# Two families of 128x128 transposes moved from the tensor engine to transposing DMAs, in a one-core layer with sorted expert rows

## What is computed

```python
xn = layernorm(x)                                   # over the 128 channels
# attention part: every token picks 8 heads x 4 points of channel indices
off = xn @ W_off + b_off                            # only off[..., 0] is used
w = softmax(xn @ W_attn + b_attn)                   # over the 4 points
idx = clip(wrap_negative(int(off[..., 0])), 0, 127)
g = take_along_axis(xn[:, 0, :], idx)               # values of token 0 of each sequence
s = sum(g * w over 32 picks)                        # one number per token
attn = broadcast(s, 128) @ W_out + b_out
# feed-forward part: 2 shared experts on all tokens, 8 routed experts, 2 per token
ffn(v, w1, w2, w3) = (silu(v @ w1.T) * (v @ w3.T)) @ w2.T      # hidden size 256
out = x + attn + sum of both shared experts + weighted sum of the 2 chosen experts
```

## Time and profile before

| | us |
|---|---|
| median of 3 runs | 472.09 |
| lowest and highest | 469.29, 472.75 |
| profiled execution, device time | 468.98 |
| its span in the profile | 467.2 |

### The profile page before, as it was taken

How to read it: one execution, slowest core, us unless ns; L and a number is a source line. 1 busy time by engine, 2 the same in 40 slices (tenths; PEclk the granted TensorE clock), 3 DMA queues, 4 the chain that set the end, 5 groups by cost and what they waited for, 6 DMA issues and landing times.

```text
span 467.2 us, 13518 instructions
## 1 busy us (share of the span) xinstructions
PE 402.0 (86%) x4741; PEld 344.9 (74%) x4741; DVE 344.9 (74%) x1093; ACT 202.7 (43%) x353; POOL 198.4 (42%) x169
## 2 busy tenths in 40 slices
PE   0554776797899999999969899999999999999990
PEld 0543634464567777777847799999999999999990
DVE  5976899979848689999998778886555555555551
ACT  3797753147222554554524334543333433333330
POOL 0432404144865434333360000001888876666664
PEclk9976898799999999999979999999999999999996
DMA  8600000010241111111120144542455554432332
GB/s 301 179 2 1 1 1 1 0 36 20 81 138 44 53 32 49 54 53 46 53 54 0 34 134 133 154 130 84 61 73 65 61 72 55 67 29 27 31 29 22
DMA packets 34998, 28.75 MB, mean 62 GB/s; under 512 B 5632, under 2 KB 28544, under 8 KB 34944
## 3 DMA queue, kind: packets, MB, share of 16 engines
q1 hardware_dynamic: 23248, 19.23, 14.3%
q0 software_dynamic: 11264, 8.69, 13.1%
q10 hardware_dynamic: 432, 0.11, 0.1%
HBM read 15.13 MB, written 12.88 MB: 60 GB/s over the span
## 4 chain that ended last, share of the span: by engine, by line
PE 72%; DVE 16%; ACT 6%; issue 3%; POOL 1%; DMA 1%; POOLq 0%; ACTq 0%; DVEq 0%
PE pY L750 16%; PE pY L576 10%; PE pAB L723 8%; PE pAB L725 7%; PE pAB L724 7%; PE pAB L561 5%; PE pAB L562 5%; PE pAB L563 5%; ACT units L788 4%; PE pV L601 3%; PE pV L588 3%; PE pV L699 2%; DVE hbuf L1079 2%; DVE hot L1233 1%; ACT xT L796 1%
## 5 line engine op out<-in xcount | busy, mean ns | idle before, releaser
L957 POOL DMA_INDIRECT out_dram<-xT,rows x64 | 99.0, 1547 | 104.5 <-DVE xT L1395 67.4
L723 PE MATMUL pAB<-hotT,wsp 128*128 128x128 f16 x620 | 108.5, 219 | 0.5
L725 PE MATMUL pAB<-hotT,wsp 128*128 128x128 f16 x620 | 108.5, 219 | 0.0
L724 PE MATMUL pAB<-hotT,wsp 128*128 128x128 f16 x620 | 108.4, 219 | 0.0
L942 POOL DMA_INDIRECT sorted_rows<-rows,slot x64 | 68.2, 1066 | 84.5 <-DVE hbuf L1079 65.9
L1344 DVE SCALAR_TENSOR_TENSOR hbuf<-pAB,units 128x512 f32<-128x512 f32 x78 | 53.7, 688 | 67.4 <-PE pAB L725 65.9
L906 ACT ACTIVATE units<-pAB 128x512 f32<-128x512 f32 x78 | 46.4, 595 | 102.9 <-PE pAB L725 102.7
L750 PE MATMUL pY<-wsp,hbuf 128*128 (+1 forms) x620 | 87.0, 282 | 1.0 <-DVE xT L1406 0.7
L852 ACT ACTIVATE units<-pAB 128x512 f32<-128x512 f32 x64 | 38.1, 597 | 114.2 <-PE pAB L563 114.2
L750 PEld LDWEIGHTS pY<-wsp,hbuf 128*128 128x128 f32 x620 | 75.6, 192 | 1.9 <-DVE hbuf L1344 0.8
L576 PE MATMUL pY<-wsp,hbuf 128*128 128x128 f32 x512 | 72.0, 286 | 0.0
(11 more groups left out here) (153 smaller groups left out, 596.4 us busy)
## 6 DMA issues: line engine op xcount, KB each, us to landing
rows<-sorted_rows SPq DMA_DIRECT2D x32, 137.0 KB, 2.4
base<-in_x SPq DMA_DIRECT2D x8, 512.0 KB, 7.4
out_dram<-base SPq DMA_DIRECT2D x16, 256.0 KB, 2.6
wraw<-in_wall SPq DMA_DIRECT2D x10, 256.0 KB, 2.8
proj<-sorted_rows SPq DMA_DIRECT2D x27, 68.5 KB, 1.9
wsp<-in_wall SPq DMA_DIRECT2D x10, 128.0 KB, 3.3
sorted_rows<-rows,slot POOLq DMA_INDIRECT x64
out_dram<-xT,rows POOLq DMA_INDIRECT x64, 3.3
```

The source lines that it names most:

```text
L723: pe.matmul(o, hi, x(0), start=True, stop=False)
L724: pe.matmul(o, hi, x(1), start=False, stop=False)
L725: mm = pe.matmul(o, lo, x(0), start=False, stop=True)
L957: pool.indirect_dma_start(out_rows, bass.IndirectOffsetOnAxis(ap=xr[:, job.step, t % 2, DEST:DEST + 1].bitcast(U32), axis=0), yt[:, t], No ...
```

## The change

All transposes after stage 1 go to DMAs with a transpose, all of them issued by SyncE.

- Stage 3: `turn_hot` and `hot_copy` are gone. For each pair SyncE issues one DMA that reads 128x1024 float16 of `hot` in SBUF and writes 8 transposed blocks to `hotT`, now 4 buffers deep (`TURNS`) and laid in `units`. Number m waits for its batch of `hot` and until picks 0 to m-4 are done. `pick` lags two units and alternates between two banks of pV; `weigh` lags two units, and `weighted_high` one. The loads of expert weights stand between these DMAs in SyncE's program.
- Stage 4: a step's load is two DMAs: the 9 words of weights and destination, and a transposing DMA of 256x256 float16 from HBM straight to `xrT`. An extra load is likewise a small one and a transposing one of 128x256. Both pairs count on the same semaphore. `r_turn` and `r_xt` are gone, the lags are 0 and 2, and the transposed rows stay for good: there is no ring. SyncE's 8-ahead rule now waits for the first products of the last job of the turn 8 back (`d_l1`), not for its transposing.

The diff, cut to what is spoken of:

```diff
         share = sb("share", [P, P], F16)
-        units = sb("units", [P, 4, 512], F32)
+        units = sb("units", [P, 6, 512], F32)
         silu = units[:, 0:2, :]
-        xs = units[:].rearrange("p r (j c) -> p r j c", j=TPB)
+        xs = units[:, 0:4, :].rearrange("p r (j c) -> p r j c", j=TPB)
+        hotT = units[:, 2:6, :].bitcast(F16)
         hbuf = sb("hbuf", [P, 4, 512], F32)
...
-        hotT = sb("hotT", [P, 2, 8 * P], F16)
         for name, a in const.items():
...
-        xr = rows[:].rearrange("p (r k) w -> p r k w", k=2)
-        xrT = hotT[:].rearrange("p i c -> p (i c)").rearrange("p (r k s c) -> p r k s c", r=RING, k=2, s=2)
-        xe = proj[:].bitcast(I32).rearrange("p t c -> p (t c)")[:, 0:EXTRAS * ROWW].rearrange("p (a w) -> p a w", w=ROWW)
+        row_words = rows[:].rearrange("p t w -> p (t w)")
+        proj_words = proj[:].bitcast(I32).rearrange("p t c -> p (t c)")
+        xr_flat = row_words[:, 0:TILES * CW].bitcast(F16)
+        xrT = xr_flat.rearrange("p (r s k c) -> p r s k c", r=MAIN_STEPS, s=2, k=2)
+        meta = row_words[:, TILES * CW:TILES * ROWW].rearrange("p (t m) -> p t m", m=META)
+        xe_flat = proj_words[:, 0:EXTRAS * CW].bitcast(F16)
+        xeT = xe_flat.rearrange("p (a s c) -> p a s c", a=EXTRAS, s=2)
+        extra_meta = proj_words[:, EXTRAS * CW:EXTRAS * ROWW].rearrange("p (a m) -> p a m", m=META)
         yt = xT[:].bitcast(F32).rearrange("p i s (t c) -> p (i s t) c", c=P)
...
-        small = sb("small", [P, RING, P], F32)
+        small = sb("small", [P, 4, P], F32)
         vscr = small[:].rearrange("p (t r) c -> p t (r c)", t=2)
...
-        xr16 = xr.bitcast(F16)
-        xr32 = xr.bitcast(F32)
-        xe16 = xe.bitcast(F16)
-        xe32 = xe.bitcast(F32)
+        meta32 = meta.bitcast(F32)
+        extra_meta32 = extra_meta.bitcast(F32)
         pV16 = pV[:].bitcast(F16)
-        pT16 = pV16[:, :, 0:4 * P].rearrange("p b (k s c) -> p b k s c", k=2, s=2)
...
             before = sum(1 if s < MAIN_STEPS else min(2, EXTRAS - 2 * (s - MAIN_STEPS)) for s in TURN_ORDER[n % AHEAD:n + 1:AHEAD])
-            eng.wait_ge(d_in[n % AHEAD], 16 * before)
-
-        def rows16_of(job, k):
-
-            return xr16[:, job.step, k] if job.main else xe16[:, 2 * job.i + k]
+            eng.wait_ge(d_in[n % AHEAD], 16 * 2 * before)
...
                 sp.dma_start(second[:, :, e, :], wall[e, :, W2:WCOL].rearrange("p (h c) -> p h c", h=2)).then_inc(w2_ready, 16)
-            with sp.Fori(1, NE // 2) as g:
-                for r in range(2):
-                    sp.wait_ge(w_split, 2 * g + r - 1)
-                    sp.dma_start(wraw[:, r, 0:W2], wall[bass.ds(2 * g + r, 1), :, 0:W2].rearrange("o p w -> p (o w)")
-                                 ).then_inc(w_in[r], 16)
+
+            def load_first(e):
+
+                sp.dma_start(wraw[:, e % 2, 0:W2], wall[e, :, 0:W2]).then_inc(w_in[e % 2], 16)
+
+            for e in range(NSH, 2 * NSH):
+                sp.wait_ge(w_split, e - 1)
+                load_first(e)
+            for m in range(APAIRS):
+                if m % 4 == 0:
+                    sp.wait_ge(hot_ready, m // 4 + 1)
+                if m >= TURNS:
+                    sp.wait_ge(v_done, m + 1 - TURNS)
+                sp.dma_start(hotT[:, m % TURNS].rearrange("p (k c) -> p k c", c=P),
+                             hot[:, m // 4 % 2, 2 * (m % 4):2 * (m % 4) + 2].rearrange("p s g b h -> p (s g b h)"),
+                             transpose=True).then_inc(hot_turned[m % TURNS], 16)
+                if m % 4 == 3 and 2 * NSH + m // 4 < NE:
+                    e = 2 * NSH + m // 4
+                    sp.wait_ge(w_split, e - 1)
+                    load_first(e)
...
                     at = nc.s_assert_within(sp.snap(tile), 0, TILES - 1, skip_runtime_bounds_check_because="clamped")
-                    sp.dma_start(xe[:, a - 1], sorted_tiles[bass.ds(at, 1)].rearrange("o p w -> p (o w)")).then_inc(landed, 16)
+                    sp.dma_start(extra_meta[:, a - 1], sorted_tiles[bass.ds(at, 1), :, CW:ROWW].rearrange("o p m -> p (o m)")).then_inc(landed, 16)
+                    sp.dma_start(xeT[:, a - 1], sorted_tiles16[bass.ds(at, 1), :, 0:2 * P].rearrange("o p c -> p (o c)"),
+                                 transpose=True).then_inc(landed, 16)
...
-                    sp.wait_ge(d_turn, n + 1 - AHEAD)
+                    sp.wait_ge(d_l1, LAST_OF_TURN[n - AHEAD] + 1)
                 if step < MAIN_STEPS:
-                    sp.dma_start(xr[:, step], sorted_steps[step]).then_inc(d_in[n % AHEAD], 16)
+                    sp.dma_start(meta[:, 2 * step:2 * step + 2], sorted_steps[step][:, :, CW:ROWW]).then_inc(d_in[n % AHEAD], 16)
+                    sp.dma_start(xrT[:, step].rearrange("p s k c -> p s (k c)"), sorted_halves[step][:, 0:2 * P],
+                                 transpose=True).then_inc(d_in[n % AHEAD], 16)
                 else:
...
-            def turn_hot(g, u):
+            def pick(g, u):
                 m = ROUND * (g - ATT) + u
-                if u % 4 == 0:
-                    pe.wait_ge(hot_ready, 2 * (g - ATT) + (u // 4 + 1))
-                if past(m, 1):
-                    pe.wait_ge(hotT_ready, m)
-                for k in range(2 * NG):
-                    mm = pe.transpose(pV16[:, 0, k * P:(k + 1) * P],
-                                      hot[:, u // 4, 2 * (u % 4) + k // NG, k % NG].rearrange("p b h -> p (b h)"),
-                                      c["ident"][:])
-                mm.then_inc(hot_turned, 1)
-
-            def pick(g, u):
-
-                m = ROUND * (g - ATT) + u
-                pe.wait_ge(hotT_ready, m + 1)
-                if past(m, 1):
-                    pe.wait_ge(v_read, m)
+                pe.wait_ge(hot_turned[u % TURNS], 16 * (2 * (g - ATT) + u // TURNS + 1))
+                if past(m, 2):
+                    pe.wait_ge(v_read, m - 1)
                 for k in range(2 * NG):
                     for s in range(2):
-                        mm = pe.matmul(pV[:, 1, k * 64:(k + 1) * 64], hotT[:, u % 2, k * P:(k + 1) * P],
+                        mm = pe.matmul(pV[:, u % 2, k * 64:(k + 1) * 64], hotT[:, u % TURNS, k * P:(k + 1) * P],
                                        table[:, bass.ds(2 * (g - ATT) + u // 4, 1), s, :].rearrange("p o c -> p (o c)"),
...
             routing = shared[:1] + [(0, routing_products, 0, UNITS)] + shared[1:]
-            both = shared[:1] + [(0, turn_hot, ROUND * ATT, UNITS), (1, pick, ROUND * ATT, UNITS)] + shared[1:]
+            both = shared[:1] + [(2, pick, ROUND * ATT, UNITS)] + shared[1:]
             straight(0, 2 * ROUND, routing)
...
-            def r_turn(g, r):
-
-                job = JOBS[UNROLL * g + r]
-                if not job.turns:
-                    return
-                rows_landed(pe, job.step)
-                if job.turn == 0:
-                    pe.wait_ge(w_split, NE)
-                if job.turn >= 2:
-                    pe.wait_ge(d_xt, job.turn - 1)
-                for k in range(2 if job.main else job.experts):
-                    for s in range(2):
-                        mm = pe.transpose(pT16[:, job.turn % 2, k, s, :], rows16_of(job, k)[:, s * P:(s + 1) * P], c["ident"][:])
-                mm.then_inc(d_turn, 1)
-                if job.turn == 0:
-                    spread_sides()
-
             def r_first(g, r):
...
-                pe.wait_ge(d_xt, job.turn + 1)
+                if q == 0:
+                    pe.wait_ge(w_split, NE)
+                    spread_sides()
+                if job.turns:
+                    rows_landed(pe, job.step)
                 if q >= 2:
...
-                        x = lambda s: xrT[:, job.turn % RING, job.t % 2 if job.main else k, s, :]
+                        x = lambda s: xrT[:, job.step, s, job.t % 2, :] if job.main else xeT[:, 2 * job.i + k, s, :]
                         for h in range(2):
...
-            def hot_copy(g, u):
-                m = ROUND * (g - ATT) + u
-                act.wait_ge(hot_turned, m + 1)
-                if past(m, 2):
-                    act.wait_ge(v_done, m - 1)
-                nc.scalar.copy(hotT[:, u % 2, :], pV16[:, 0, :]).then_inc(hotT_ready, 1)
-
             def routed_high(g, u):
...
-            def r_xt(g, r):
-
-                job = JOBS[UNROLL * g + r]
-                if not job.turns:
-                    return
-                act.wait_ge(d_turn, job.turn + 1)
-                if job.turn == 0:
-                    act.wait_ge(v_done, APAIRS)
-                if job.turn >= RING:
-                    act.wait_ge(d_l1, LAST_OF_TURN[job.turn - RING] + 1)
-                n = 2 if job.main else job.experts
-                nc.scalar.copy(xrT[:, job.turn % RING, 0:n], pT16[:, job.turn % 2, 0:n]).then_inc(d_xt, 1)
-                if job.turn == 0:
-                    act.wait_ge(sides_done, 1)
```

(36 more changed lines are left out.)

6 lines of the change are left out of this document (1 added, 5 removed).

## The result

| | before | after |
|---|---|---|
| median, us | 470.92 (469.29 to 472.75, 4 runs) | 479.24 (478.48 to 479.59, 4 runs) |
| profiled execution, its span | 468.98, 467.2 | 479.59, 477.5 |
| ratio after to before | | 1.0173, 95% interval 1.0126 to 1.0221 |

The account below looks back on a forecast made before the run. TensorE was taken to set the pace in stages 3 and 4; gains of 8.0 us (stage 3) and 10.1 us (stage 4), 18.1 in all, off 470.8 gave 452.7, stated as 452.5 us. Range 444 to 550, the likeliest case's own 444 to 461.

Parts of the forecast that it names:

- the DMA part: Bounds on the added transposing DMAs in stages 3 and 4: 1.9 to 2.9 us a pair, hidden, costing nothing.
- the turning point: Stage 4's extra turns: SyncE's issue time per transposing DMA above which it would turn bad, 0.95 us.
- the extra turns: Stage 4, 14 turns of extra tiles: 0.22 us saved each; SyncE 2.2 us behind, covered by 18 us head start.
- Stage 3: One-hot transposes leave TensorE and VectorE sets the pace at 3.0 us in units 36 to 59: 8.0 us gained.
- the seam: Passage from stage 3 to stage 4: a copy and a turn saved on the chain, the copy put at zero.
- the stall: Stage 3 near 236 us: TensorE's 4.64 us wait beside GpSimd's memsets stays, with 1.0 us of gain lost.
- The main turns: Stage 4, turns of the 32 steps: 0.22 us saved each, part of 10.1 us for 46 turns.
- It still catches up with its backlog: Stage 4: GpSimd's sends at 1.85 us a tile stay under a 2.29 us job, so they take no gain away.
- rival 1: Small transposing pieces are dear and stage 3 runs at the DMA's pace: 475 us or more, up to 564; chance 0.22.
- Rival 2: Blocks of one transposing DMA go one after another, in stages 3 and 4: 595 us or more; chance 0.10.
- rival 3: Stage 3 gives nothing, VectorE's in-order waits holding units at 3.18 us: 460.7 us; chance 0.08.
- Rival 4: DMAs keep up, but the first step or extra turns are 8 to 18 us late: about 466 us; chance 0.08.

Follow-up runs that it names:

- Experiment 2: The kernel before with only the change's stage 4 part (sorted rows transposed by the DMA that loads them): 485.17 us, ratio 1.030.
- experiment 3: The kernel after, with only the 27 extra loads plain again and their tiles turned by TensorE: 461.01 us, ratio 0.978.
- experiment 5: The kernel after, with extra loads' tile numbers as constants instead of register reads by SyncE (other tiles, same size): 468.8 us, ratio 0.994.
- experiment 1: The kernel before with only the change's stage 3 part (one-hot tiles transposed by DMA): 464.84 us, ratio 0.985.
- Experiment 4: The kernel after, with the 16 output blocks issued by ScalarE's queue instead of SyncE's: 474.03 us, ratio 1.003.

## Why the prediction was wrong

**The step that failed** is the last of the DMA part: "with two transposing issues at 0.38 that is 2.45 us against 2.29 for a job". The 0.38 was the issue time of an ordinary load, given without bounds to an operation that the trace did not have, while the DMA engines' time for the same operation had been bounded from both sides. Measured are 1.18 to 1.34 us. The working behind it was right as far as it went: it put the turning point at 0.95 us (0.94 by its own terms), and 1.19 is over it. By the same formula the extra turns would have been (18 + 14 x 2.29 - 14 x (1.69 + 2.38)) = -6.9, 6.9 us late; what it lacked is that a load then takes 2.18 us with its register and plain part, and a turn with a block about 5. With these, 2 x (2.18 - 1.19) + 0.57 = 2.55 us a turn beside the transposing issues, the turning point would be an estimated (18 + 14 x 2.29 - 14 x 2.55) / 28 = 0.5 us; no run has a transposing issue shorter than 1.17 us to show where it lies. From the second products at 297.0 to those at 328.1 six jobs took 5.2 us each. Experiment 2 puts the loss into stage 4, experiment 3 into these 27 loads, and experiment 5 into SyncE's time for them.

**Stage 3: right, but for the seam.** 8.0 us forecast, 6.7 measured by experiment 1. By the unit starts in the two profiles, units 36 to 59 with the stall took 83.3 us before (162.61 to 245.94) and 78.2 after (162.09 to 240.31): 5.1 gained, where 5.5 - 1.0 = 4.5 was forecast, at 3.03 us a unit instead of 3.0. The stall cost 5.60, the 1.0 more that was foreseen. One pick waited for its transposes, 0.8 us. The other eight units gave 1.3 of the 3.5 us forecast: 2.4 in units 32 to 35, but -1.1 from unit 60 to the first routed product, where one pick more stands now (0.47 us). There TensorE also waited 0.73 us for a weighing and 1.64 for VectorE's last sum of the shared part, 0.17 and 0.65 before. The weighings now lag one unit more, and VectorE has no pause before them. No experiment was made on it. The prediction had put the seam at zero.

**The main turns: right in kind, too large.** 32 x 0.22 = 7.0 forecast; experiment 3 against 1 gives 464.84 - 461.01 = 3.8. Behind the 22nd job the 56 main jobs took 134.3 us in the profile of experiment 1 (318.6 to 452.9) and 129.9 in that of 3 (317.6 to 447.5), 4.4 less where 28 x 0.22 = 6.2 was to be expected. The price of a turn is not what was wrong. The earlier trace rows compares an extra job with a main one, but main jobs alone show the same in the kernel before; every other one has a turn:

```profile
401.17 1.11 PE L750 MATMUL pY<-wsp,hbuf 128*128 x8
403.46 1.11 PE L750 MATMUL pY<-wsp,hbuf 128*128 x8
405.97 1.11 PE L750 MATMUL pY<-wsp,hbuf 128*128 x8
408.26 1.11 PE L750 MATMUL pY<-wsp,hbuf 128*128 x8
```

These are 2.29, 2.51 and 2.29 us apart. Without turns most jobs of experiment 3 take 2.28 to 2.31, but not all: some take up to 2.41, one 3.49 (3.35 in experiment 1) and one 3.04 (2.77). So some 1.8 us were given back in other places; why is open.

**The extra turns: wrong in sign.** 14 x 0.22 = 3.1 us gained were forecast, 18.2 lost. The three measured terms, -6.7 - 3.8 + 18.2, make 479.24 - 471.56 = +7.7 by the way they were taken; that they do is no check. The check that they can be taken one by one is experiment 2.

**"It still catches up with its backlog": wrong.** GpSimd's 1.85 us is under a job's 2.29, but the backlog's size hangs on when the first send may go, and that is the last output block in SyncE's queue. From 353.87 the 64 sends last until 472; TensorE's last second products were at 463. Experiment 4 took this alone away: the tail behind the last second products (461.3 there) was 11.6 us again instead of 14.35. It is 2.7 of the 18.2 us.

**Rivals.** The time, 479, lies inside the range and in the region of rival 1, but not by its mechanism: 82,224 packets took 28.9% of the 16 engines, 27 ns each, and in the stretch of the waits the DMA share was 0.29. Rival 2 did not happen, nor rival 3. Rival 4 was the right mechanism: an issue over its threshold, and the extra turns late. Its price of "8 to 18 us" late fits the 15.6 and 18.2; its time of 466 took 13 of them off the forecast's gain, where the extra turns cost 18.2 + 3.1 = 21.3 against the forecast, the main turns 3.2 and stage 3 1.3. It had a chance of 0.08 because 0.38 had been taken for the issue.

**The two rules of the Trainium skill.** "Advanced Engine Details and Errata", section "X-Bar Transpose (TRN2)", says transposing DMAs are as fast as ordinary ones. In the DMA engines' time that held: 1.7 to 1.9 us a pair, where the prediction had worked out 1.9 from the ordinary loads, though not under the microsecond the prediction read into it. For the issuing engine it did not hold: 1.19 us against 0.35. The Trainium skill's 1309 ns for a block, in "VectorE: DVE Perf Modes", section "The three transpose paths", are not a price per block here, since 8 blocks were turned every 3.2 us.

## What to carry to other kernels

A transfer has three prices: the time of the engine that issues it, the time of the DMA engines, and its landing. When a change adds a new kind of DMA, bound each of the three, and for the first count every instruction of the issuing queue between two deadlines, register reads included. A transposing DMA's issue hardly depends on its size, so use few large ones (here one of 256 KB every 3.2 us held up one pick by 0.8 us, two of 64 KB every 2.3 us cost 18), and leave small ones with a close deadline to the tensor engine. Look too at what stands behind them in the queue: here the output blocks, and behind those the first send.
